# A fused four-layer network on one core: the tokens' expert shares reach the inner rows by DMA instead of by selection matmuls

## The reference, cut to what matters

```python
probs = softmax(xf @ Wgate + expert_bias)
topk_p, topk_i = top_k(probs, 2); topk_p = topk_p / sum(topk_p)
comb = sum(one_hot(topk_i, 8) * topk_p[..., None], axis=1)     # a token's share in each expert
g, u = silu(xf @ Wg[e]), xf @ Wu[e]                            # for every expert e
routed = sum_e comb[:, e] * ((g * u) @ Wd[e])
out = shared_expert(xf) + routed
```

## Time and profile before

| | |
|---|---|
| three runs, us | 1758.2, 1757.12, 1752.28; median 1757.12 |
| span of the profiled execution, us | 1746.6 |
| median less span, us | 10.5 |
| PE busy | 1377.0 us (79%) |
| DVE busy | 950.6 us (54%) |
| ACT busy | 699.9 us (40%) |
| stage L2f | from 1330.7 to 1412.1 us |
| stage L3f | from 1590.3 to the end |

### The profile page before, as it was taken

The page is one execution under the profiler, slowest core; times in us unless marked ns, Lnnn a source line. Parts: engine busy times, 40 slices in busy tenths (PEclk is TensorE's granted clock), DMA queues, the critical chain, the costliest instruction groups (busy, mean ns, idle before and its releaser), DMA issues. The chain is left out here.

```text
span 1746.6 us, 25267 instructions
## 1 busy us (share of the span) xinstructions
PE 1377.0 (79%) x9006; PEld 777.6 (45%) x9006; DVE 950.6 (54%) x2159; ACT 699.9 (40%) x1885; POOL 461.9 (26%) x585
## 2 busy tenths in 40 slices
PE   3677854858999969756886798988887968887998
PEld 2333423625555636443332456565653333332333
DVE  6545561145555654255454667676774754554654
ACT  3232431337566534333333565555642233343221
POOL 1000033154423352341001385858450001000000
PEclk8676876989999988887898799899897977987999
DMA  2433001150000002221000000000000010000000
GB/s 49 119 118 116 13 37 61 32 118 7 7 1 1 2 25 78 83 60 21 8 3 2 0 1 1 1 1 1 1 1 0 1 22 8 9 2 1 7 7 12
DMA packets 66993, 45.31 MB, mean 26 GB/s; under 512 B 17564, under 2 KB 60262, under 8 KB 66870
## 3 DMA queue, kind: packets, MB, share of 16 engines
q1 hardware_dynamic: 61013, 34.48, 7.4%
q0 software_dynamic: 4096, 8.40, 1.9%
q10 hardware_dynamic: 1760, 0.82, 0.3%
HBM read 24.91 MB, written 13.89 MB: 22 GB/s over the span
## 5 line engine op out<-in xcount | busy, mean ns | idle before, releaser
L3265 ACT ACTIVATE L2a_pr<-psum,L2a_negmax 128x512 f32<-128x512 f32 (+3 forms) x256 | 131.7, 525 | 131.2 <-DVE L2a_negmax L3335 72.7
L551 ACT ACTIVATE L1x_praw<-psum,L1x_negmax 128x154 f32<-128x154 f32 x256 | 95.9, 390 | 76.2 <-DVE L1x_negmax L643 75.9
L3133 PE MATMUL psum<-ident,L2a_pr 128*128 128x128 f32 x640 | 95.7, 299 | 34.0 <-DVE L2a_pT L3355 20.0
L312 POOL TENSOR_TENSOR L1x_pm<-L1x_praw,L1x_total 128x1024 f32<-128x1024 f32 x32 | 60.7, 1898 | 156.5 <-DVE L1x_total L649 105.6
L3133 PEld LDWEIGHTS psum<-ident,L2a_pr 128*128 128x128 f32 x640 | 80.2, 155 | 41.1 <-issue 25.1
L1536 DVE TENSOR_REDUCE L0x_negmax<-psum 128x6 f32<-128x924 f32 (+1 forms) x48 | 47.7, 1010 | 80.7 <-PE psum L1066 77.7
L1536 DVE TENSOR_REDUCE L2x_negmax<-psum 128x6 f32<-128x924 f32 (+1 forms) x48 | 47.7, 1011 | 63.0 <-PE psum L1066 53.1
L1536 DVE TENSOR_REDUCE L3x_negmax<-psum 128x6 f32<-128x924 f32 (+1 forms) x48 | 47.8, 1011 | 62.6 <-PE psum L1066 53.6
L643 DVE TENSOR_REDUCE L1x_negmax<-psum 128x4 f32<-128x616 f32 x64 | 50.7, 794 | 52.9 <-PE psum L364 49.3
L2253 POOL DMA_INDIRECT slots_in<-L0f_pair,L0f_to x16 | 15.6, 975 | 224.5 <-DVE L0f_to L2242 216.7
L3024 POOL TENSOR_TENSOR L2a_pr<-L2a_pr,L2a_total 128x1024 f32<-128x1024 f32 x32 | 60.6, 1895 | 51.4 <-DVE L2a_total L3363 51.4
(11 more groups left out here) (732 smaller groups left out, 3455.1 us busy)
## 6 DMA issues: line engine op xcount, KB each, us to landing
expert_arena<-in_L_ffn_w SPq DMA_DIRECT2D x16, 256.0 KB, 5.3
group_in<-zero SPq DMA_DIRECT2D x2, 1472.0 KB, 11.2
L1f_xs<-group_in SPq DMA_DIRECT2D x10, 256.0 KB, 4.6
group_out<-L1f_ys SPq DMA_DIRECT2D x10, 256.0 KB, 2.3
L1f_gu<-in_L_ffn_gate_up_w SPq DMA_DIRECT2D x8, 256.0 KB, 3.9
slots_in<-zero SPq DMA_DIRECT2D x1, 1280.0 KB, 9.8
L0f_xs<-slots_in SPq DMA_DIRECT2D x5, 256.0 KB, 4.3
resid<-in_x SPq DMA_DIRECT2D x4, 256.0 KB, 6.0
```

The source lines that it names most:

```text
L312: nc.gpsimd.tensor_tensor(pm[:, n % 2].rearrange("p j t k -> p (j t) k"), praw[:, n % 3, :, :, 0:MAIN].rearrange("p j t k -> p (j t) k"), ...
L551: nc.scalar.activation(praw[:, n % 3, j, t, :], psum[:, 2 * u + j, x * CTX:(x + 1) * CTX], ACT.Exp, bias=negmax[:, n % 2, u, j, x:x + 1], ...
L3133: last = nc.tensor.transpose(psum[:, TURN + n // 4, n % 4 * P:(n % 4 + 1) * P], pr[:, m % RING, n * P:(n + 1) * P], core.ident[:])
L3265: ins = nc.scalar.activation(pr[:, i % RING, SEQ * j + lo:SEQ * j + hi], psum[:, bank + j, lo:hi], ACT.Exp, bias=negmax[:, i % RING, e:e + ...
```

## The change

The shares stay f32: `weights` writes `comb` and no split, `sharesT` turns `comb` with the f32 identity, ACT writes `shares` [NC, 2, 512] in f32. SP then copies, for each share column c of a pair, the two rows c and c + 1 of `shares` onto 128 partitions of `wide` (64 copies of each row), and for column 16 the one row onto all 128. Each column has a semaphore of its own, and `wide` two buffers by batch. DVE's `hid` reads `wide` in place of PSUM and waits for that semaphore. The selection matmuls, the bf16 parts and GpSimd's matrices are gone. In L2f the shared unit, which needs no share, moves from the last to the first place of the batch.

```diff
-    SPREAD, RESULT, OUT, ROUTE = 4, 5, 6, 7
+    RESULT, OUT, ROUTE = 5, 6, 7
+    cols = sorted({x[3] for x in units if x[3] is not None})
+    spread_in = {c: nc.alloc_semaphore(f"{L}_spread_in{c}") for c in cols}
...
-        split = sb("split", [P, QT, 3, NC], BF16)
-        shares = sb("shares", [K3, 2, SEQ], BF16)
...
+        shares = sb("shares", [NC, 2, SEQ])
+        wide = sb("wide", [P, 2, len(cols), SEQ])
...
+                def spread(f):
+
+                    sp.wait_ge(s["shares"], f + 1)
+                    for c in sorted(cols, key=first_use.get):
+                        if f:
+                            sp.wait_ge(spread_in[c], 16 * f)
+                        if f >= 2:
+                            sp.wait_ge(s["hid"], NU * (f - 2) + last_use[c] + 1)
+                        held = 1 if c == E else 2
+                        sp.dma_start(wide_of(f, c), shares[c:c + held, f % 2, :].unsqueeze(1).to_broadcast([held, P // held, SEQ])).then_inc(spread_in[c], 16)
...
+                spread(0)
+                for f in range(1, B):
+                    if final is not None and f >= 2:
+                        store(f - 2)
+                    spread(f)
...
-            @block.gpsimd
-            def _(pool):
...
                 def sharesT(f):
                     pe.wait_ge(s["share"], f + 1)
                     for t in range(QT):
-                        last = nc.tensor.matmul(psum[0:K3, ROUTE, t * P:(t + 1) * P], split[:, t].rearrange("p k e -> p (k e)"), identb[:],
-                                                start=True, stop=True)
+                        last = nc.tensor.transpose(psum[0:NC, ROUTE, t * P:(t + 1) * P], comb[:, t, :], core.ident[:])
...
-                def spread(n):
-                    b, (_, _, rows, col, _) = n // NU, units[n % NU]
-                    if n % NU == 0:
-                        pe.wait_ge(s["shares"], b + 1)
-                    if n:
-                        pe.wait_ge(s["hid"], n)
-                    if col is not None:
-                        sel = alone[:, 0:rows] if col == E else wide[:, col:col + 2, :].rearrange("p e i -> p (e i)")
-                        nc.tensor.matmul(psum[0:rows, SPREAD, :], sel, shares[:, b % 2, :], start=True, stop=True).then_inc(s["spread"], 1)
...
                 def shared(f):
                     act.wait_ge(s["share_ps"], f + 1)
-                    nc.scalar.activation(shares[:, f % 2, :], psum[0:K3, ROUTE, :], ACT.Copy).then_inc(s["shares"], 1)
+                    if f >= 2:
+                        for c in cols:
+                            act.wait_ge(spread_in[c], 16 * (f - 1))
+                    nc.scalar.activation(shares[:, f % 2, :], psum[0:NC, ROUTE, :], ACT.Copy).then_inc(s["shares"], 1)
...
-                    dve.wait_ge(s["spread"], n // NU * GATED + gated(u) + 1)
-                    nc.vector.tensor_tensor(hid[0:rows, n % 3, :], half[0:rows, n % 2, :], psum[0:rows, SPREAD, :], ALU.mult).then_inc(s["hid"], 1)
+                    b = n // NU
+                    dve.wait_ge(spread_in[col], 16 * (b + 1))
+                    nc.vector.tensor_tensor(hid[0:rows, n % 3, :], half[0:rows, n % 2, :], wide_of(b, col)[0:rows, :], ALU.mult).then_inc(s["hid"], 1)
...
-        items = [pair(w["wg"], w["wu"], w["wd"], i) for i in range(4)]
-        items.append((w["wg"][:, 8, :], w["wu"][:, 8, :], 64, None, w["wd"][0:64, 4, :]))
+        items = [(w["wg"][:, 8, :], w["wu"][:, 8, :], 64, None, w["wd"][0:64, 4, :])]
+        items += [pair(w["wg"], w["wu"], w["wd"], i) for i in range(4)]
```

More of the change, by code:

```diff
@@ L1794, in experts @@
     s = {n: nc.alloc_semaphore(f"{L}_{n}") for n in (
-        "var", "sd", "vec", "gate_up", "up", "silu", "spread", "hid", "down", "outT", "out", "const", "sel", "ready",
+        "var", "sd", "vec", "gate_up", "up", "silu", "hid", "down", "outT", "out", "ready",
         "share", "share_ps", "shares", "sum")}
+    cols = sorted({x[3] for x in units if x[3] is not None})
+    spread_in = {c: nc.alloc_semaphore(f"{L}_spread_in{c}") for c in cols}
     stored = [nc.alloc_semaphore(f"{L}_stored{b}") for b in range(B)]
     r, oh, eq, score, gap = router.s, router.oh, router.eq, router.score, router.gap
-    K3 = 3 * NC
+    first_use = {c: [x[3] for x in units].index(c) for c in cols}
+    last_use = {c: max(u for u, x in enumerate(units) if x[3] == c) for c in cols}
     with ExitStack() as scope:
@@ L1808, in experts @@
         comb = sb("comb", [P, QT, NC])
-        rest = sb("rest", [P, 2, QT, NC])
-        split = sb("split", [P, QT, 3, NC], BF16)
-        shares = sb("shares", [K3, 2, SEQ], BF16)
[L1812 to L1815, removed]
+        shares = sb("shares", [NC, 2, SEQ])
+        wide = sb("wide", [P, 2, len(cols), SEQ])
         acc = sb("acc", [P, QT, D])
@@ L1825, in experts, with wide_of @@
         stats_v, stats_s = rows_rstd(core, L, s["var"], s["sd"], rms=x1 is not None)
-        n_const = 3 + (extra == "sigmoid")
+        def wide_of(b, c):
+            return wide[:, b % 2, cols.index(c), :]
         with nc.Block() as block:
@@ L1831, in _, with store @@
             def _(sp):
+                def spread(f):
[7 more added lines that the diff above has]
+                        sp.dma_start(wide_of(f, c), shares[c:c + held, f % 2, :].unsqueeze(1).to_broadcast([held, P // held, SEQ])).then_inc(spread_in[c], 16)
+                def store(b):
+                    sp.wait_ge(s["ready"], b + 1)
+                    sp.dma_start(final[b].rearrange("(t p) d -> p t d", p=P), last_rows[b % 2][:]).then_inc(stored[b], 16)
+                spread(0)
[3 more added lines that the diff above has]
+                    spread(f)
                 if final is not None:
-                    for b in range(B):
-                        sp.wait_ge(s["ready"], b + 1)
-                        sp.dma_start(final[b].rearrange("(t p) d -> p t d", p=P), last_rows[b % 2][:]).then_inc(stored[b], 16)
+                    for b in range(B - 2, B):
+                        store(b)
                     for b in range(B):
                         sp.wait_ge(stored[b], 16)
-            @block.gpsimd
-            def _(pool):
[L1843 to L1850, removed]
             @block.tensor
@@ L1855, in rowsT @@
                 def rowsT(f):
+                    pe.wait_ge(s["shares"], f)
                     pe.wait_ge(r["gap"], f)
@@ L1909, in _ @@
                         up(n + 1)
-                        spread(n + 1)
                     if b and u == 0:
@@ L1989, in weights @@
                     v.done()
+                    if f:
+                        dve.wait_ge(s["share_ps"], f)
                     if extra == "sigmoid":
                         v.step(nc.vector.tensor_scalar(comb[:, :, E], gap[:, 1, :], 0.5, 0.5, ALU.mult, ALU.add))
-                    v.step(nc.vector.tensor_tensor(comb[:, :, 0:E], eq[:], score[:], ALU.add))
-                    v.done()
-                    if f:
-                        dve.wait_ge(s["share_ps"], f)
-                    v.step(nc.vector.tensor_copy(split[:, :, 0, :], comb[:]))
-                    v.done()
-                    v.step(nc.vector.tensor_tensor(rest[:, 0], comb[:], split[:, :, 0, :], ALU.subtract))
-                    v.done()
-                    v.step(nc.vector.tensor_copy(split[:, :, 1, :], rest[:, 0]))
-                    v.done()
-                    v.step(nc.vector.tensor_tensor(rest[:, 1], rest[:, 0], split[:, :, 1, :], ALU.subtract))
-                    v.done()
-                    nc.vector.tensor_copy(split[:, :, 2, :], rest[:, 1]).then_inc(s["share"], 1)
+                        v.done()
+                    nc.vector.tensor_tensor(comb[:, :, 0:E], eq[:], score[:], ALU.add).then_inc(s["share"], 1)
                 def product(n):
@@ L2039, in finished @@
                                                        op0=ALU.mult, op1=ALU.add).then_inc(s["ready"], 1)
-                GATED = sum(x[3] is not None for x in units)
-                def gated(u):
-                    return sum(x[3] is not None for x in units[:u])
                 weights(0)
```

2 lines of the change are left out of this document (removed).

## The result

| | before | changed |
|---|---|---|
| time, median us | 1757.66 (4 runs, 1752.28 to 1761.75) | 2032.91 (4 runs, 2021.41 to 2034.42) |
| ratio, 95% interval | | 1.1561 [1.1533, 1.1589] |
| span of the profiled execution | 1746.6 | 2032.6 |
| chain that ended last | PE | SP's queue and the copies (9% and 7% of the span) |

The forecast was 1820 with a range of 1785 to 1935. The sign was right and the size far off: +275 us where +63 was forecast. The time is 98 us above the upper end of the range.

The account below looks back on a forecast made before the run. Copies on two DMA engines, 5.4 us a pair, were to replace PE as the bound: L3f +41 us, L2f +18.6 and about 1, span 1807.6, plus 10.5 gives 1818, given as 1820; range 1785 to 1935.

Parts of the forecast that it names:

- Number of engines: Share copies of both stages: a pair's copy runs on 2 DMA engines, 64 packets of 2 KB on each.
- Time of one copy (T): Share copies of both stages: one pair's copy of 64 packets per engine takes 5.4 us.
- the second price (7.7): A rival for the pair copy: 0.12 us a packet, T = 7.7 us, 1928 us in all; chance 0.24.
- the third (14.4): A rival for the pair copy: 0.225 us a packet, T = 14.4 us, 2250 us in all; chance 0.05.
- The packet price itself: Share copies: a 2 KB packet takes its engine 0.084 us, from a transfer of 32 rows onto 8 partitions.
- The sum over the stages: Copies run without a break and set stage length: L3f +41 us, L2f +18.6 and about 1; together +61, span 1807.6.
- Each us of T is worth 48 us: Scaling of the total with one pair copy's time, from 32 copies in L3f and 16 in L2f.
- The 10.5 us that the prediction put on top of the span: What the median holds over the profiled span, added to span 1807.6 to give 1818 us.
- What is removed: 16 selection matmuls in L2f and 44 in L3f, 0.31 us each: 18.6 us off PE.
- rival 3: All 16 engines run, a copy takes 0.9 us and is hidden, PE stays the bound: 1739 us; chance 0.08.
- Start of the stages: Before the first copy of each stage: no splits, f32 turning put at 1.0 us, shares some 0.8 us earlier in L3f.
- Half clock (rival 4): PE at half clock all through both stages, its work doubled: +116 us more, 1935 us; chance 0.05.

Follow-up runs that it names:

- experiment 1: Changed kernel with each pair's copy made as two copies, one source row onto 64 partitions each, so sixteen engines work; 1984.2 us, one run.
- experiment 2: Changed kernel with the two source rows of a pair 16 partitions apart, still two engines, column 16 read from two places; 1826.66 us, one run.
- experiment 5: Changed kernel with the two source rows of a pair 32 partitions apart, still on 2 engines; 2053.74 us, one run.
- experiment 6: Changed kernel with the shares one partition higher, so pairs are read from partitions 1 and 2, 3 and 4 and so on; 1987.74 us, one run.
- experiment 7: Changed kernel without any copies, `wide` filled with 1.0 once, so the output leaves out the shares; 1723.3 us, ratio 0.9801 to the kernel before.
- experiment 4: Changed kernel with each pair read from eight rows, 4 partitions apart, on 8 engines; 1724.66 us, ratio 0.9824 to the kernel before.

## Why the prediction was wrong

- **Number of engines: right.** Two small packets, share 0.12, through both stages. Two engines were not what it cost, though: experiment 1 uses sixteen and gains 2%.
- **Time of one copy (T): the step that failed.** It priced a packet at 0.084 us from the earlier trace rows, gave each of the two engines its own stream, and called the slower rows cases of "eight engines that crowd onto eight neighbouring partitions, where two writers have the way to themselves". It looked for crowding on the written side alone. The crowd is on the read side: both rows of every pair stand in the same group of four partitions, which gives 25 to 27 GB/s in all (experiments 1, 2, 5 and 6). T is 9.8 to 10.0 us and not 5.4; it lay between the second price (7.7) and the third (14.4), and the range ended at the second.
- **The packet price itself: right.** With the rows on different groups T is 5.27 us (experiment 2), and the run takes 1827 us. The source's place is worth at least the 206 us between that and the changed kernel, since that run's column 16 costs its two engines more.
- **The sum over the stages: right.** "Each us of T is worth 48 us": 32 x (9.8 - 5.4) + 16 x (10.0 - 5.4) = 214 us, and 1820 + 214 = 2034, against 2033 measured. This T is read from the run itself, so it tests the form of the sum alone. By parts, the last `hid` of L3f should end at 1801 + 214 = 2015 and ends at 2026; 6.8 of these 11 us are there before L2f has its first shares (`comb` ends at 1341.4, before at 1334.6). The 10.5 us that the prediction put on top of the span make up for this: they are no cost outside the span, since the run of 2034.39 us has a span of 2032.6, but what the profiled execution of the kernel before was faster than the median.
- **What is removed: mis-sized.** 18.6 us was the term; without copies the kernel is 28 to 42 us faster (experiment 7). A product is worth 0.49 to 0.52 us in L3f and 0.22 in L2f, not 0.31 in both. The timeline held the answer for L3f: gate is 0.86 from its start to the next and up, the same matmul, 0.96. This did not touch the forecast, in which PE no longer ends last, but rival 3 should have been near 1727, the 30 us of experiment 4 below 1757, and not 1739.
- **Start of the stages: right, with luck in the clock.** The bf16 turning of 0.60 us in the earlier trace rows ran at a granted clock of 0.50. At that clock f32 takes 1.01 (L2f), as forecast, and the shares start 1.10 us after `comb` ends where it was 1.87: a gain of 0.8, as forecast. In L3f the turning found the clock at 1.00 and took 0.61, and the gain was 1.3 us (0.70 for 2.00).
- **Half clock (rival 4): it came in part, and cost next to nothing.** PE is busy about half the time, and the granted clock is 0.57 to 0.71 in most stretches, between the levels of 1.2 and 2.4 GHz; the down matmul at 1709.23 takes 2.08 us for 1.02. With a copy every 10 us PE has the time for it, and behind the last pair's `hid` the stage needs 8.7 us more, where 8 was put.

The trace of the kernel before had a transfer that hints at this, and the prediction doesn't use it. In attention one row is repeated onto the other side as well (L907); its issue on SP's queue, the stretch in which it runs, and that stretch's packets:

```profile
1416.57 0.54 SPq L907 DMA_DIRECT2D L3x_k<-ones  x1
```

```profile
1417.75:1418.95 1.20, 0.66 (x4) 0.42 (x4) 0.84 (x5) 1.00 (x2) 0.00 (x0) 0.99 0.17 24
```

```profile
DMA packets 91, 0.03 MB, mean 24 GB/s; under 512 B 91, under 2 KB 91, under 8 KB 91
```

A share of 0.17 is 2.7 engines on average, and they move 24 GB/s together. With that row as the price of a repeated source a copy of 256 KB takes 10.9 us, and the sum gives 2084; the two-engine packet price was taken from transfers whose 32 source rows lie on many groups. But its packets are of 320 bytes (80 numbers), not of 2 KB, and it writes four partitions, so at the time it could as well have been a price of small packets. It was reason for a rival, not for a certain figure.

What stays open: why eight engines from eight places move 136 GB/s, 17 each, where four move 25 each; and what the written side does, which no run varied.

## What to carry to other kernels

Price a transfer from two counts at least, and take the lower rate: the engines (small packets in the trace), and the groups of four partitions that it reads. Of the groups that it writes these runs say little; the first transfer of the earlier trace rows wrote onto two of them at 164 GB/s for 0.4 us, so the price of reading can't simply be carried over. A repeated source is the case where the second is easily missed: to spread a row by DMA, first hold it on several groups (four places and four engines made the same 256 KB go from 9.8 us to 2.6), and the copies then hide behind matmuls. A busy DMA share is no sign of speed; look at the GB/s beside it. And when a matmul is removed, price it by what a unit becomes without it, comparing like matmuls from start to start, not by its own distance to the next, and look whether the engine then waits for something else, as PE does in L2f.

## What the runs showed of the hardware that had not been expected

- Reading is bound by group: 25 to 27 GB/s from one group with 2 engines, 27 with 16; 50 from two groups; 100 from four; 136 from eight. Partitions 3 and 4 are in different groups, 1 and 2 in one, p and p + 32 in one, p and p + 16 in two.
- The rate of one group is the same for 1 KB and 2 KB packets (26 GB/s).
- Where PE is the bound, a single bf16 product between f32 matmuls costs it 0.52 us, a second one beside it 0.22.
- Turning the shares takes PE 0.60 us in f32 and 0.39 in bf16 at the full granted clock, 1.01 and 0.59 at half.
